# One broadcast load of v as four transfers of 32 partitions in an RWKV-plus-attention kernel

## The reference

```python
# layer 0: RWKV block; 32 heads (h) of 16 channels (s_)
xa = ln(x);  sx = shift(xa) - xa
xxx = tanh((xa + sx * maa_x) @ maa_w1)             # five low-rank mixes
xm = xa + sx * (maa_stack + xxx @ maa_w2)          # inputs of k, w, v, r, g
w = exp(-exp(time_decay + tanh(xw @ td_w1) @ td_w2))
r, k, v = xr @ Wr.T, xk @ Wk.T, xv @ Wv.T;  g = silu(xg @ Wg.T)
def step(s, rkvw):                                  # scan over the 128 time steps
    a = k_t[..., :, None] * v_t[..., None, :]
    out = einsum('bhi,bhij->bhj', r_t, u * a + s)
    s = a + w_t[..., :, None] * s
x1 = x + group_norm(out) * g @ Wo.T
xc = ln(x1); ...                                    # channel mix: Wfr, Wfk, Wfv
# layer 1: instance norms, three 128x128 projections, softmax attention 512x512
A = softmax(Mn.T @ Mm);  y = Wo @ (Ml @ A.T) + bo + x
```

## Time and profile before

| what | value |
|---|---|
| runs | 1008.86, 1010.12, 1018.79 us; median 1010.12 us |
| the profiled execution | 1013.51 us, span 1011.8 us, mean granted TensorE clock 0.938 of full speed |
| PE busy | 897.9 us, 89% of the span |
| DVE busy | 686.1 us, 68% |
| POOL busy | 531.0 us, 52% |
| ScalarE busy | 388.0 us, 38% |
| DMA | 100.33 MB, mean 99 GB/s; SP's queue 87.08 MB, ScalarE's 12.59 MB |

### The profile page before, as it was taken

How to read it: one execution, slowest core, us unless ns; L and a number is a source line. 1 busy time by engine, 2 the same in 40 slices (tenths; PEclk the granted TensorE clock), 3 DMA queues, 4 the chain that set the end, 5 groups by cost and what they waited for, 6 DMA issues and landing times.

```text
span 1011.8 us, 10530 instructions
## 1 busy us (share of the span) xinstructions
PE 897.9 (89%) x3588; PEld 401.8 (40%) x3588; DVE 686.1 (68%) x875; ACT 388.0 (38%) x755; POOL 531.0 (52%) x573
## 2 busy tenths in 40 slices
PE   3789699999889984995989997999889999899998
PEld 1234233443334331442434444443343444444454
DVE  5345489899789975775979997787896424443342
ACT  2034113332234211311424634552363444937394
POOL 1001486788848868367889986886866101010100
PEclk9799898899979987897999998999888999999999
DMA  7182328354854527244365130534201212010101
GB/s 271 21 187 93 119 80 178 121 162 114 175 167 141 153 80 144 75 131 144 111 155 145 33 101 25 155 89 137 59 9 33 82 62 84 0 42 0 42 1 41
DMA packets 92984, 100.33 MB, mean 99 GB/s; under 512 B 21891, under 2 KB 63107, under 8 KB 90883
## 3 DMA queue, kind: packets, MB, share of 16 engines
q1 hardware_dynamic: 86018, 87.08, 32.6%
q10 hardware_dynamic: 6912, 12.59, 3.4%
HBM read 65.05 MB, written 33.55 MB: 97 GB/s over the span
## 4 chain that ended last, share of the span: by engine, by line
PE 53%; DMA 16%; DVE 10%; POOL 6%; issue 5%; ACT 5%; SPq 4%; ACTq 0%; DVEq 0%; POOLq 0%
PE PS L1357 34%; DMA VB<-scr_vs 10%; PE PS L1486 4%; PE PS L1590 3%; PE PS L1366 3%; PE PS L1424 2%; SPq L497 2%; DMA scr_v<-STG 2%; PE PS L1567 2%; DVE M L1070 2%; DMA scr_g<-STG 2%; PE PS L1501 2%; POOL VB L753 2%; DVE VB L1186 2%; POOL VB L745 2%
## 5 line engine op out<-in xcount | busy, mean ns | idle before, releaser
L1357 PE MATMUL PS<-M,W 128*128 128x512 f32 x544 | 267.2, 634 | 16.4 <-DVE M L1070 12.4
L745 POOL TENSOR_TENSOR VB<-KR,VB 128x1008 f32<-128x1008 f32 x64 | 129.1, 2017 | 116.5 <-PE PS L1486 66.9
L1186 DVE TENSOR_TENSOR_SCAN VB<-PS,VB 128x512 f32<-128x512 f32 x128 | 149.0, 1206 | 40.0 <-POOL VB L753 38.0
L1357 PEld LDWEIGHTS PS<-M,W 128*128 128x128 f32 x544 | 103.4, 201 | 156.9 <-issue 138.2
L753 POOL TENSOR_TENSOR VB<-VB 128x1008 f32<-128x1008 f32 x64 | 150.6, 2353 | 3.5
L1067 DVE TENSOR_TENSOR VB<-VB,PS 128x2048 f32<-128x2048 f32 x64 | 146.0, 2282 | 2.0
L749 POOL TENSOR_TENSOR VB<-WG,VB 128x1008 f32<-128x1008 f32 x64 | 128.2, 2003 | 0.1
L633 POOL TENSOR_SCALAR NM<-MV 128x2 f32<-128x2 f32 (+1 forms) x24 | 5.3, 225 | 232.6 <-DVE MV L1314 147.4
L1357 PE MATMUL PS<-W,M 128*128 128x512 f32 x224 | 107.3, 605 | 0.0
L1486 PE MATMUL PS<-VB,HEAD 128*32 128x512 f32 x512 | 72.5, 640 | 19.5 <-DVE VB L1067 19.2
L1332 DVE TENSOR_REDUCE SM<-PS 128x1 f32<-128x512 f32 x64 | 43.4, 687 | 58.3 <-PE PS L1590 57.5
(11 more groups left out here) (176 smaller groups left out, 1312.4 us busy)
## 6 DMA issues: line engine op xcount, KB each, us to landing
VB<-scr_vs SPq DMA_DIRECT2D x16, 1024.0 KB
W<-in_w SPq DMA_DIRECT2D x8, 1024.0 KB, 9.1
scr_vs<-STG SPq DMA_DIRECT2D x64, 64.0 KB, 5.0
scr_v<-STG SPq DMA_DIRECT2D x16, 256.0 KB, 6.6
scr_w<-STG ACTq DMA_DIRECT2D x16, 256.0 KB, 5.1
scr_k<-STG ACTq DMA_DIRECT2D x16, 256.0 KB, 2.7
KR<-scr_k SPq DMA_DIRECT2D x16, 256.0 KB, 4.3
WG<-scr_w SPq DMA_DIRECT2D x16, 256.0 KB, 5.0
```

Source lines behind the costliest of these rows:

```text
L745: po.tensor_tensor(vo, KO[:, 0:N2 - 1].unsqueeze(1).to_broadcast([P, S, N2 - 1]), VB[:, 2 + s, 0, :, 1:N2], ALU.mult).then_inc(g_kv, 1)
L1186: sc = dv.tensor_tensor_scan(s_, PS[:, 5, :], b_, 0.0, ALU.mult, ALU.add)
L1357: mm = pe.matmul(o, l, r, start=i == 0, stop=i == 3)
```

## The change

The one transfer of line 544 becomes four, one for each group of 32 partitions. Each has 32 rows of 8 KB as its outermost dimension on both sides, reads the same 256 KB of `scr_vs`, and adds 16 to the same semaphore; POOL waits for 64 per load in place of 16. Bytes, places and the order of the steps are unchanged.

```diff
@@ stream_load, line 543
-                    src = vs_rows[q, bb % QB].unsqueeze(0).to_broadcast([4, H, S * L])
-                    sp.dma_start(VB[:, 2 + s].rearrange("p s j n -> p (s j n)"), src).then_inc(d_vb[s], 16)
+
+                    for c in range(4):
+                        sp.dma_start(VB[H * c:H * c + H, 2 + s].rearrange("p s j n -> p (s j n)"),
+                                     vs_rows[q, bb % QB]).then_inc(d_vb[s], 16)
@@ POOL, stream_scan, line 741
-                    w.wait_ge(d_vb[s], 16 * (bb // 2 + 1))
+                    w.wait_ge(d_vb[s], 64 * (bb // 2 + 1))
```

## The result

The changed kernel takes 950.79 us (median of four runs, 947.6 to 961.08), the kernel before 1010.0 us in the same comparison: ratio 0.9414, 95% interval 0.9322 to 0.9505. The forecast was 945 us, range 905 to 985.

What follows compares the result with a forecast made beforehand. The prediction took the load of v, confined to four DMA engines, to hold up TensorE: 51.7 us of waits plus 23.2 of low clock, less 10 given back, made 65 us off, 945 us against a median of 1010.1; range 905 to 985.

Steps and rivals of the forecast that it cites:

- The cause: Load of v at line 544: four copies outermost confine it to four of the 16 DMA engines, share 0.23.
- The size of the load's landing: Load of v after the change: 3.7 us transfer, 1.8 issues, 2.0 fixed part, 7.5 us; bounds 5.7 to 19.0.
- The waits: Seven waits of TensorE between 100 and 780 us, traced back to loads of v, 51.7 us; 10 us given back.
- The clock: TensorE's clock at 1.2 GHz for a while behind each of the seven waits: 23.2 us of lost work regained.
- the ledger: List of TensorE's seven waits traced to loads of v, with the low clock behind them: 74.9 us together.
- The sum: Whole kernel: 74.9 us of waits and low clock less 10 given back, 65 us off.
- A: Scan stretch: early loads, stores and staging slots also remove half of the remaining losses, 102 us off, 908 us; chance 15%.
- B: Load of v: transfers to 32 partitions get half the width, load lands after 11.2 us, kernel 960 us; chance 16%.
- C: Scan: DVE or the loop through POOL, DVE and PE gives back half the gain, 977 us; chance 13%.
- D: Load of v: quarters go one behind the other, landing after 19.0 us, at most 7 us off, 1003 us; chance 6%.
- E: Load of v: four transfers still use four engines and added issues cost time, slower at 1023 us; chance 5%.
- The marks: Trace signs: share near 0.8, v within 12 us, r about 5, no PE wait over 6, clock 0.96, DVE 72%.

Runs made afterwards that it cites:

- e5_two: Against the kernel before, each load of v made as two transfers of 64 partitions, two copies outermost in each; 1122.07 us, ratio 1.1101.
- e9_outer4: Against the kernel before, one 1 MB load of v with four outermost at a real stride, no repeated source; 1005.47 us, ratio 0.9987.
- e10_outer8: Against the kernel before, one load of the same bytes with eight outermost, strided source rows; 959.68 us, ratio 0.9545.
- e7_quarter: Against the changed kernel, only the first quarter of each load, 256 KB, made from batch 2 on; 946.29 us, ratio 0.937 to the kernel before.
- e4_wide: Against the changed kernel, one 1 MB load with 128 different rows outermost replaces the four; 948.67 us, ratio 0.9414 to the kernel before.
- e11_again: The changed kernel unaltered, measured once more for a narrower interval; 945.65 us, ratio 0.9404 to the kernel before.

## Why the prediction was right, step by step

**The cause.** Right, and shown by e5_two, e9_outer4 and e10_outer8: with two, four and eight outermost the DMA share is that of 2.1, 3.5 and 8.2 engines.

**The size of the load's landing.** Forecast 7.5 us from the first issue. A quarter lands 7.5 us after its own issue (median), the last one is issued about 1.4 us after the first (358.56 and 359.98 us for one load), so near 8.9 us, an estimate: 1.4 too little. The rate was the mis-sized term: 284 GB/s was taken from a wide load, and 220 was had, which is 1.1 us more for 1.049 MB. An added issue cost 0.42 us, not 0.586. The range's upper bound of 19.0 us was far off; the quarters overlap, since four landings of 4.3 us one behind the other would take 17.2.

**The waits.** Forecast: all seven close whole, 51.7 us, and 10 us are given back. Measured: 40.1 us closed, and on balance nothing given back elsewhere. The discount was of the right size for the wrong reason. It should not have been 1.4 us at each place; four closed to under 1.2 us, and 4.17 + 6.04 of the 11.6 us stayed at two that hang on stores and SP's order. That the sum came out is in part luck. The chain of the changed kernel shows why (start, duration, what), the first three lines for the first place, the last for the second:

```profile
253.27 0.61 ACT STG L831
...
253.89 0.55 SPq L497
...
255.79 6.87 DMA scr_o<-OT
...
364.05 11.90 DMA scr_v<-STG
```

The issues of line 497 wait for a copy by ScalarE, and the store of the output stands behind them on SP and then takes 6.87 us. At the second, the store of v is issued behind the four loads of v (from 358.56 us) and lands after 11.90 us; e7_quarter and e4_wide, where the load holds the engines for less time, shorten that wait.

**The clock.** Forecast 23.2 us; busy time fell by 20.0. Behind the two waits that stayed 10.0 us of the 23.2 remain, so 13.2 came from the seven places and some 6.8 from stretches that the ledger hadn't listed. Windows of one microsecond show them: some 11 us less are lost behind other waits (around 172, 612, 701, 748 and 769 us before), and 4.5 us more in two stretches of the changed kernel at 18 and 70 us, before its first load of v. In e11_again the low clock costs 20.9 us in the whole span where it costs 27.1 here. So 20.0 beside the forecast 23.2 is near for the wrong reason, and part of that 6.8 may be no more than what differs between two executions of one kernel.

**The sum.** Forecast 65 us in the profiled execution, measured 60.2 (1013.51 to 953.33 us by execution, 1011.8 to 951.6 by span). By the terms, the idle time gave 40.2 where 51.7 - 10 = 41.7 were forecast, and the clock 20.0 where 23.2 were. But e11_again, by the same reckoning, gained 68.9 us, so the 5 us lie within the difference between two executions of the changed kernel.

**The rivals.** A (102 us) asked for half of the rest; of the idle time, 62.2 us before and 62.1 after, nothing went. Its 54 us of clock were also too many: part of the low clock falls in time in which PE is idle and costs nothing, and by windows of one microsecond 41 us fell in busy time. B is half right, above. C (DVE takes over) didn't come: DVE's share went to 72% as worked out, and its wait for POOL's sums fell from 38.0 to 14.2 us. By time alone the forecast and B can't be told far apart: 945 and 960 us are ratios of 0.936 and 0.950, and the 0.9365 to 0.9444 of e11_again lies between them. D and E fell with the landing, 7.5 us a quarter; the rule quoted beside D doesn't carry over, since the one transfer that the four replace ran on four engines. For E, e5_two shows the mechanism it needed, transfers that stay on few engines, at 1.11.

**The marks.** The share of 0.94 in a load was above the 0.8 expected; PE's clock of 0.97 and DVE's 72% came as said. Missed: the longest landing of a quarter was over 12 us (15.2 for one), the load of r took 7.8 us and not 5, one wait of PE was over 6 us, by 0.04, and SP's 11.8 us at line 497 are halved, not gone: four issues take 5.27 us at 365.44.

## What to carry to other kernels

Look at the DMA share in a stretch where one large transfer is alone in flight: if it is 4/16 and the outermost dimension is 4, rewrite the access as transfers with at least 16 rows outermost. It brought 6% here, at three more issues per load (16 is the smallest number tried, in eight transfers at a time; nothing between 8 and 16 was). Price it not by the time it frees on the DMA engines but by a ledger of TensorE's waits: follow each back to the transfer, or to what stands behind the transfer in the same queue, and add the slow-clock stretch that each wait leaves behind. The ledger told eight loads from eight others here, with 33 and 19 us forecast where 37 and 17 were measured, and next to nothing for the other eight, which brought 5.

## What the runs showed of the hardware that I hadn't expected

A wait that is cut to a half can keep the other part of its price whole: 12.72 us and 6.04 us of idle time were both followed by ten microseconds at a mean clock of 0.50. The halved wait gave back its idle half and nothing of the clock. Nor does the price follow the length in other traces: in windows of two microseconds PE lost 2.5 us to the low clock behind the wait of 11.44 us, and 3.4 us behind the 2.14 us of e4_wide.

And the DMA share can be full at well under the rate: 315, 224 and 179 GB/s per full share for 128, 32 and 16 partitions a transfer, over the same 1573 KB. The share alone would have called these three the same.
